# One launch of a base product, a gated LoRA and a low-rank layer: setup work of four engines put in a new order, the last stores split, and the first 128 columns of W cast by VectorE

## The reference

```
base   = x @ W.T                                   # W 1024 x 1024
logits = x @ Wr.T + 5 * one_hot(id of the sequence)  # 8 experts
gates  = softmax over the top 2 logits, 0 elsewhere
h      = x @ A_e.T  for each expert e, rank 16     # 8 x 16 = 128 columns
c      = base + 2 * sum_e gates_e * (h_e @ B_e.T)
out    = x + c @ (U * S @ V.T).T                   # rank 256: U 1024 x 256, V 1024 x 256
```

## Time and profile before

| what | us |
|---|---|
| median of three runs | 159.39 (159.06, 159.39, 841.72) |
| the profiled execution | 159.01 |
| its span, first to last instruction | 157.4 |
| PE busy in it | 150.8 |
| DVE, POOL, ACT busy | 104.2, 69.7, 65.2 |

### The profile page before, as it was taken

The page is one execution under the profiler, slowest core; times in us unless marked ns, Lnnn a source line. Parts: engine busy times, 40 slices in busy tenths (PEclk is TensorE's granted clock), DMA queues, the critical chain, the costliest instruction groups (busy, mean ns, idle before and its releaser), DMA issues.

```text
span 157.4 us, 2558 instructions
## 1 busy us (share of the span) xinstructions
PE 150.8 (96%) x884; PEld 140.6 (89%) x884; DVE 104.2 (66%) x298; ACT 65.2 (41%) x148; POOL 69.7 (44%) x53
## 2 busy tenths in 40 slices
PE   7999998999699999999999999999999999999990
PEld 6999998999498999989998999899989989998880
DVE  0798956364977269958396657938692968397861
ACT  4697681519444641452255115512450542233200
POOL 2000041085926923067715953593659067701800
PEclk9999999999999999999999999999999999999998
DMA  5999999994043075039418942874580077006076
GB/s 189 324 398 410 394 410 409 409 380 162 0 135 116 18 207 171 26 135 328 150 73 306 340 139 107 299 257 141 216 282 39 0 278 255 4 23 249 1 294 239
DMA packets 10669, 32.72 MB, mean 208 GB/s; under 512 B 1440, under 2 KB 2208, under 8 KB 10528
## 3 DMA queue, kind: packets, MB, share of 16 engines
q1 hardware_dynamic: 10368, 32.16, 55.9%
q10 hardware_dynamic: 288, 0.39, 0.7%
HBM read 24.16 MB, written 8.39 MB: 207 GB/s over the span
## 4 chain that ended last, share of the span: by engine, by line
PE 76%; DMA 7%; SPq 5%; POOL 4%; ACT 2%; DVE 2%; issue 1%; DVEq 0%
PE pj L313 15%; PE pj L315 15%; PE pj L314 15%; PE fin L313 10%; PE fin L314 9%; PE fin L315 9%; DMA w_raw<-in_W 7%; POOL xT_lo L269 2%; PE zt L378 2%; SPq L218 2%; POOL vw_raw L279 2%; DVE w_lo L694 2%; SPq L192 1%; ACT vw_raw L571 1%; PE gt L360 1%
## 5 line engine op out<-in xcount | busy, mean ns | idle before, releaser
L269 POOL TENSOR_TENSOR xT_lo<-xt_raw,xT_hi 128x1024 fp32r<-128x1024 f32 x16 | 41.1, 2568 | 56.8 <-ACT xT_hi L565 56.8
L313 PE MATMUL pj<-proj_hi,xT_hi 128*128 128x392 f32 x128 | 45.0, 351 | 0.1
L315 PE MATMUL pj<-proj_hi,xT_lo 128*128 128x392 f32 x128 | 43.6, 340 | 0.0
L314 PE MATMUL pj<-proj_lo,xT_hi 128*128 128x392 f32 x128 | 43.5, 340 | 0.0
L284 POOL TENSOR_TENSOR x_all<-x_all,vw_raw 128x512 f32<-128x512 f32 x18 | 22.9, 1291 | 17.6 <-DVE vw_raw L798 17.6
L313 PE MATMUL fin<-v_hi,w_hi 128*128 128x256 f32 (+1 forms) x84 | 27.0, 321 | 0.6 <-DVE w_lo L694 0.5
L315 PE MATMUL fin<-v_hi,w_lo 128*128 128x256 f32 (+1 forms) x84 | 26.4, 314 | 0.0
L314 PE MATMUL fin<-v_lo,w_hi 128*128 128x256 f32 (+1 forms) x84 | 26.4, 314 | 0.0
L313 PEld LDWEIGHTS pj<-proj_hi,xT_hi 128*128 128x128 f32 x128 | 24.0, 188 | 1.3 <-POOL xT_lo L269 0.3
L314 PEld LDWEIGHTS pj<-proj_lo,xT_hi 128*128 128x128 f32 x128 | 24.1, 188 | 0.5
L315 PEld LDWEIGHTS pj<-proj_hi,xT_lo 128*128 128x128 f32 x128 | 24.0, 188 | 0.0
(11 more groups left out here) (87 smaller groups left out, 231.9 us busy)
## 6 DMA issues: line engine op xcount, KB each, us to landing
xt_raw<-in_xt SPq DMA_DIRECT2D x16, 512.0 KB, 4.0
x_all<-in_x SPq DMA_DIRECT2D x16, 512.0 KB, 5.5
out<-x_all SPq DMA_DIRECT2D x14, 512.0 KB, 3.1
vw_raw<-in_VW SPq DMA_DIRECT2D x6, 384.0 KB, 6.7
w_raw<-in_W SPq DMA_DIRECT2D x8, 256.0 KB, 10.0
u_raw<-in_U SPq DMA_DIRECT2D x1, 1024.0 KB, 13.1
out<-x_all SPq DMA_DIRECT2D x3, 256.0 KB, 3.3
aw_raw<-in_AW SPq DMA_DIRECT2D x1, 544.0 KB, 7.9
```

Source lines behind the costliest of these rows:

```text
L269: nc.gpsimd.tensor_sub(xT_lo[:, t % 2, :, :], xt_raw[:, t % XTR, :, :], xT_hi[:, t % 2, :, :].bitcast(F32)).then_inc(xt_lo, 1)
L313: nc.tensor.matmul(dst, l_hi, r_hi, start=first, stop=False, skip_group_check=shared)
L314: nc.tensor.matmul(dst, l_hi, r_lo, start=False, stop=False, skip_group_check=shared)
L315: return nc.tensor.matmul(dst, l_lo, r_hi, start=False, stop=last, skip_group_check=shared)
```

## The change

- **Loads (SP).** W's second half (8 loads) is issued in one block ahead of A/Wr, x tile 0 and B. Before, two of them went first and the others between these.
- **Start.** PE does 7 products with zeros, not 8. DVE casts the first 128 columns of W's chunk 0 as its first instruction, with a semaphore of its own (`w_first_hi`), beside ACT's cast of V; ACT had done it behind V.
- **ACT and DVE in phase 1.** A/Wr's cast and subtraction move from behind chunk 9 to behind chunk 12, x tile 0's cast from behind chunk 12 to behind chunk 13.
- **Around step 1.** ACT casts x tile 2 before y, and ghT_hi(0) before us_hi(0). DVE does ghT_lo(0) before us_lo(0), and us_lo(1) only behind the gates of tile 1 and the split of z, in front of ghT_lo(1). POOL subtracts x tile 2 before the first two tsums; tsum 1 is now made in the first group and tsum 2 in the second.
- **tl.** DVE's first split of tsum moves from the end of step 3 to the end of step 2; its waits follow the new numbering.
- **Stores.** Tile 12 is stored in two halves, each as soon as its additions are done, with tile 13 between them.

```diff
+        w_first_hi = sem("w_first_hi")
...
-            load_w(0)
-            load_w(1)
+            for k in range(OC):
+                load_w(k)
             sp.dma_start(aw_raw[:, :, :], AW).then_inc(aw_load, 16)
             load_xt(0)
-            load_w(2)
-            load_w(3)
             sp.dma_start(b_raw[:, :, :], B).then_inc(b_load, 16)
-            for k in range(4, OC):
-                load_w(k)
             load_xt(1)
...
-            store_pair(PAIRS - 2)
+            p = PAIRS - 2
+            sp.wait_ge(fin_read, READS * (p - 1) + 4)
+            sp.dma_start(out_v[2 * p, :, 0:BANK], x_all[:, (2 * p) % XR, 0:BANK]).then_inc(stored[(2 * p) % XR], 16)
+            sp.wait_ge(fin_read, READS * (p - 1) + 5)
+            sp.wait_ge(side_add, ADDS * (p - 1) + 3)
+            sp.dma_start(out_v[2 * p + 1, :, :], x_all[:, (2 * p + 1) % XR, :]).then_inc(stored[(2 * p + 1) % XR], 16)
+            sp.wait_ge(fin_read, READS * (p - 1) + 6)
+            sp.dma_start(out_v[2 * p, :, BANK:D], x_all[:, (2 * p) % XR, BANK:D]).then_inc(stored[(2 * p) % XR], 16)
...
                 if j == 3:
-                    pool.wait_ge(tsum_done, 3)
+                    pool.wait_ge(tsum_done, 2)
...
             split_x(0)
             split_x(1)
+            split_x(2)
             pool.wait_ge(y_done, 2)
             make_tsum(0)
-            make_tsum(2)
-            split_x(2)
+            make_tsum(1)
             split_x(3)
             pool.wait_ge(gh_done, 3)
-            make_tsum(1)
+            make_tsum(2)
             make_tsum(3)
...
-                    if m < 2:
-                        pe.wait_ge(w_hi_done, m + 1)
+                    if m == 0:
+                        pe.wait_ge(w_first_hi, 1)
+                    if m == 1:
+                        pe.wait_ge(w_hi_done, 1)
...
-            for n in range(8):
+            for n in range(7):
...
                 if i == 0:
-                    nc.scalar.copy(w_hi[:, 0, 0:P], w_chunk(0)[:, 0:P]).then_inc(w_hi_done, 1)
...
-                act.wait_ge(tsum_done, 3 + b)
+                act.wait_ge(tsum_done, 2 * b + 2)
...
-                if i == OC + 1:
+                if i == OC + 4:
                     act.wait_ge(aw_load, 16)
...
-                if i == OC + 4:
+                if i == OC + 5:
                     split_x(0)
...
             exp_top(0)
+            split_x(2)
             act.wait_ge(s_load, 16)
...
+            split_gh(0)
             split_us(0)
-            split_gh(0)
-            split_x(2)
             split_us(1)
...
+            dve.wait_ge(vw_load[0], 16)
+            nc.vector.tensor_copy(w_hi[:, 0, 0:P], w_chunk(0)[:, 0:P]).then_inc(w_first_hi, 1)
...
-                if i == OC + 1:
+                if i == OC + 4:
                     dve.wait_ge(aw_hi, 1)
...
+            split_gh(0)
             split_us(0)
-            split_gh(0)
-            split_us(1)
             gates_top(1)
             gates_apply(1)
             split_za(0)
+            split_us(1)
             split_gh(1)
```

More of the change, by code:

```diff
@@ L252, in _ @@
             for j in range(XR):
-                n = len(range(j, TILES, XR)) + (2 if j == LAST % XR else 1 if j == (LAST - 1) % XR else 0)
+                n = len(range(j, TILES, XR)) + (2 if j == LAST % XR else 1 if j in ((LAST - 1) % XR, (LAST - 3) % XR) else 0)
                 sp.wait_ge(stored[j], 16 * n)
@@ L692, in split_w @@
             def split_w(i):
-                dve.wait_ge(w_hi_done, i + 2)
+                if i == 0:
+                    dve.wait_ge(w_first_hi, 1)
+                dve.wait_ge(w_hi_done, i + 1)
                 nc.vector.tensor_sub(w_lo[:, i % WRING, :], w_chunk(i),
@@ L835, in step @@
                     split_gh(s)
+                    split_t(0)
                 elif s == 3:
@@ L839, in step @@
                     split_gh(s)
-                    split_t(0)
                     split_t(1)
```

## The result

158.26 us, median of 14 runs (157.47 to 158.99), against 159.19 for the kernel before in the same rounds: a ratio of 0.994 (95% interval 0.9918 to 0.9962), some 0.95 us faster and well within 2%. The forecast was 157.7 (155.9 to 159.0) and 1.4 us gained by its sum. The median lies in the range, and 0.06 us above the main band of 157.0 to 158.2. The profiled execution of the changed kernel took 158.99, the slowest of its 14, with a span of 157.2, so its trace shows only 0.2 us less span than before.

The account below looks back on a forecast made before the run. PE, busy almost throughout at full clock, bounds the kernel, so time comes only from its pauses and both ends. 1.0 + 0.4 = 1.4 us off 159.01 gives 157.6, taken as 157.7; range 155.9 to 159.0.

Parts of the forecast that it names:

- main band: Whole kernel: the forecast's main case, a time of 157.0 to 158.2 us, chance 0.55.
- Chunks 12 to 15: Phase 1: PE's pause ahead of chunk 13 goes, nothing replaces it by 0.05 us at chunk 14; gain 0.76 us.
- (b): PE's pause ahead of chunk 13, 24.13 to 24.90: 0.76 us with the restart, predicted to go.
- ghT_lo(0) first: Around step 1: pauses (c) and (d) go; with (b), step 2 would start at 40.6, 2.65 us earlier.
- (c): PE's pause ahead of the mix of step 1, 39.63 to 41.30: 1.56 us with the restart, predicted to go.
- (d): PE's pause ahead of step 2, 42.80 to 43.26: 0.33 us, predicted to go.
- us_lo(1) behind the gates: Mix of step 2: us_lo(1) stands behind POOL's split, so the mix waits from 45.1 to 46.65; net gain 1.0 us.
- DVE wins the tie: Rival at step 1: us_lo(1) ends at 44.1, the whole 2.65 us stay, 156.0 to 156.3; chance 0.22.
- Stores: Kernel's end: without a backlog the last 128 KB land in less than 2.4 us; gain taken 0.4, bounds 0 and 0.7.
- Zeros and first cast: Kernel's start: gain 0, since chunk 2's start at 8.32 is set by the DMA of its own data.
- Clock: Rival in the first chunks: the clock rises only behind chunk 2, giving 159.7, slower than before; chance 0.07.
- a sign of being wrong: PE's first chunks: the prediction is wrong if product spacing of 0.21 us goes on behind 6.5.

Follow-up runs that it names:

- 0.71 alone: Kernel before with only the new order of loads and new places of the A/Wr and x tile 0 work: 158.45 us, 0.9961.
- step 1 alone: Kernel before with only the new ScalarE, VectorE and GpSimd order around step 1 and the tsum order: 158.66 us, 0.9971.
- delayed GpSimd: Changed kernel plus a useless ScalarE copy ahead of the cast of x tile 3, VectorE's order untouched: 157.04 us, 0.9881.
- the exchange: Changed kernel with us_lo(1) straight behind the gates of tile 1, ahead of the split of z: 156.53 us (0.9853), later 156.83 (0.9868).

## Why the prediction was right, and where it was off
*Chunks 12 to 15.* Right: pause (b) went, POOL's split came second behind w_lo(13) and held w_lo(14), and the room at chunk 14 was as thin as reckoned (0.34 us of pause in one trace). Predicted 0.76; in PE's starts 0.71 alone, with chunk 2 0.13 late in that trace, and 0.6 us in time. What the prediction left out is that the pause (b) had also hidden late landings (the table above).

*ghT_lo(0) first.* Right: (c) and (d) are gone in the changed kernel, and PE gained 1.90 us between steps 0 and 2 (from 0.10 to 2.00) in the kernel with step 1 alone, where the prediction had 1.89.

*us_lo(1) behind the gates.* Right, and the part that mattered: the near tie was read as 0.08 us from the trace before and is 0.09 in the changed kernel. The stall ended where it was put: step 2's start to its mix was 5.88 us (47.56 - 41.68), predicted 6.05. That the lock is taken by the one that starts first, the runs with delayed GpSimd and with the exchange show by turning it. The Trainium skill (SBUF — State Buffer, SBUF: two separate sides) also says that of a VectorE operation with two SBUF inputs and a GpSimd operation that reads SBUF the one that starts first gets the shared pair for the whole instruction. The traces agree: us_lo(1) takes 1.22 us when it is first and 3.38 when it is second. The rival "DVE wins the tie" was therefore not the changed kernel, but it gave the better one: predicted 156.0 to 156.3, measured 156.5 to 156.8. Its 0.22 was too much. All five traces that have this order of the two engines (changed, start, loads and stores undone, step 1 alone) have POOL first by 0.08 to 0.09 us and show the pause of 1.4 us. The lead was small, but it was no toss-up: from trace to trace it moved by less than 0.01 us.

*Stores.* Taken 0.4. The queue did empty and the last store landed 0.4 us sooner, as reckoned, but the step from there to the kernel's time failed: the span shows 0.3, and the time outside it takes 0.2 of that back. This is the term that was sized most wrongly, 0.4 for 0.1.

*Zeros and first cast.* The value, 0, fits the run with the start undone, within its interval. The sentence that 8.32 "is set by that DMA" is right in kind, since PE started chunk 2 some 1.7 us behind its landing in seven traces, before and changed among them, but it takes the landing as fixed, and that moved by up to 1.3 us between executions. In the changed kernel's profile it hid the whole gain (+1.03 of it).

*Clock.* The rival didn't come about in the changed kernel's trace, though its place was real: there products are 0.12 us apart from 5.22 on. In three other traces with the same start they stay at 0.21 longer, until 6.71 (the exchange's first, and loads undone) and 6.98 (stores undone), which the prediction had named as a sign of being wrong. The number of zeros doesn't set it: with eight of them the wide spacing ended between 5.1 and 6.6. The costly form, chunk 1 at the lower level, shows only in the trace with the start undone, behind a late load. The exchange's trace:

```profile
5.43 1.05 PE L339 MATMUL fin<-v_lo,w_hi 128*128 128x256 f32 x4
6.28 0.90 PE L344 MATMUL fin<-v_hi,w_lo 128*128 128x256 f32 x4
7.02 0.28 PE L317 MATMUL fin<-v_hi,w_hi 128*128 128x256 f32 x1
```

Chunk 1 then starts at 7.02, and chunk 2 at 8.44 right behind it, where its data were ready at 8.14 (the end of DVE's `w_lo`). So the late rise costs little, but not nothing: at most some 0.25 us, an estimate from the stores-undone trace, where the data were ready at 8.19 and chunk 2 started at 8.60, less 0.16 that a start behind a wait costs (0.06 to the start and 0.1 in the first product). The Trainium skill (TensorE: Matmul & The Clock Gate, The HAM clock gate) has the moment of the rise vary between runs, by 0.5 us either way; the traces agree that it varies, but with more between them: 1.5 us for these two.

*The rest of the gap.* Predicted 1.4, measured 0.95. The forecast of 157.7 lay even 1.7 below the 159.39 of the three first runs. As far as one trace of each kernel shows, the stores account for 0.3. Another 0.2 is the pace of the later steps: in the changed kernel's trace each step from 4 on takes 0.03 us more than in the trace before (6.36 in place of 6.33 for the short ones), until step 9, where the trace before falls into the same pace. This isn't the new order of step 1, although step 1 alone shows it too: the trace with the stores undone has the new order and keeps 6.33 to the end. The granted clock was 1.00 at either pace. What decides between the two paces stays open.

## What to carry to other kernels
When two engines exclude each other, the order in which two instructions start is worth their whole length: look for near ties (here 0.09 us deciding 1.4) and turn them by exchanging neighbours in one queue. Take work off the path only after asking what waits behind it in its new place; us_lo(1) cost 0.4 us ahead of the gates and 1.4 behind them. A pause that is taken away may have absorbed late loads, so the kernel behind it follows every late landing. A shorter span is not yet a shorter time: compare what lies outside it as well. Before a single trace is read for a difference of half a microsecond, compare the landings of the first loads in it with other traces.

## What was not expected of the hardware
- The load of chunk 2 (384 KB, the third that SP issues) took between 4.7 and 6.0 us from issue to landing in 13 traces with the same loads ahead of it.
- An added ScalarE copy of 0.28 us made the kernel 0.9 us faster than the changed one.
- TensorE's rise from 0.21 to 0.12 us per 128x256 product came at 5.2 in one trace and at 6.7 in another with the same instructions up to there.
- With one more store in SP's program, 0.38 us in place of 0.04 passed between SP's last wait and the branch behind it, and the time outside the span grew by 0.2 us.
- The same steps of PE ran at two paces 0.03 us per step apart at the same granted clock, within one trace as well.
